# Gathering neighbour rows in a four-layer graph network: from bursts of tiles to pairs of transfers

## What is computed

```python
h = jnp.maximum(_layernorm(x, axis=-1), 0.0)   # before each layer
x = x + _L0_gnn_ref(h, adj, L0_gnn_kernel)     # normalised adjacency @ h @ W, relu
x = x + _L1_gnn_ref(h, adj, L1_gnn_W, L1_gnn_b)  # three propagations, then a linear layer
x = x + _L2_gnn_ref(h, adj, nodemask, ...)     # quantiles over the neighbours, then an MLP
x = x + _L3_gnn_ref(h, adj, L3_gnn_weight, L3_gnn_bias)  # adj @ (h @ W) + bias
```

```python
sv = jnp.sort(jnp.where(valid[..., None], x[:, None, :, :], big), axis=2)
for tau, wt in zip([0.25, 0.5, 0.75], [0.25, 0.5, 0.25]):
    pos = jnp.clip(tau * (mf - 1.0), 0.0)          # mf: number of neighbours
    agg += wt * (gather(floor(pos)) * (1 - frac) + gather(ceil(pos)) * frac)
```

## Time and profile before

| what | value |
|---|---|
| time, median of 3 runs | 2798.1 us (2797.18 to 2803.76) |
| the profiled execution | 2827.46 us, its span 2825.7 us |
| mean granted TensorE clock in it | 0.701 of full speed |
| busy: DVE, PE, Pool, PEld, ACT | 1625.1, 1535.0, 1299.3, 858.3, 462.6 us |
| Pool's gathers, L403 | 1152, 1287.4 us busy, 1118 ns mean |
| queue of the gathers (software) | 36864 packets, 37.82 MB |
| the chain of work that ended last | DVE 40%, PE 24%, "issue" 18%, unknown queue 15% |

### The profile page before, as it was taken

The page is one execution under the profiler, slowest core; times in us unless marked ns, Lnnn a source line. Parts: engine busy times, 40 slices in busy tenths (PEclk is TensorE's granted clock), DMA queues, the critical chain, the costliest instruction groups (busy, mean ns, idle before and its releaser), DMA issues.

```text
span 2825.7 us, 24253 instructions
## 1 busy us (share of the span) xinstructions
PE 1535.0 (54%) x8885; PEld 858.3 (30%) x8997; DVE 1625.1 (58%) x2443; ACT 462.6 (16%) x756; POOL 1299.3 (46%) x1196
## 2 busy tenths in 40 slices
PE   3735637556374655638366464836636375565232
PEld 2412414323142332314233241423314243233111
DVE  2511827649285574928467383755828376494926
ACT  3101212102021120202112020210302121020000
POOL 1072370735527173552717447172643707265550
PEclk9766658667586766759577676866768586777555
DMA  3122130313213131321313123131322313112120
GB/s 99 54 25 53 46 55 21 75 11 86 19 40 62 24 75 12 83 22 34 67 20 77 15 53 54 29 69 8 88 18 50 55 22 75 10 23 20 23 24 4
DMA packets 106610, 120.13 MB, mean 43 GB/s; under 512 B 71486, under 2 KB 71614, under 8 KB 106430
## 3 DMA queue, kind: packets, MB, share of 16 engines
q0 software_dynamic: 36864, 37.82, 14.2%
q1 hardware_dynamic: 69566, 79.98, 9.2%
HBM read 109.27 MB, written 8.45 MB: 42 GB/s over the span
## 4 chain that ended last, share of the span: by engine, by line
DVE 40%; PE 24%; issue 18%; another core or an unknown queue 15%; ACT 2%; DVEq 1%; POOL 0%; DMA 0%; POOLq 0%; ACTq 0%; SPq 0%
PE ps_tr L596 7%; DVE lists L1181 4%; DVE slots L1001 4%; PE ps_tr L604 4%; DVE slots L1000 3%; PE ps_prod L615 3%; PE ps_tr L585 2%; PE ps_misc L775 2%; DVE slots L1008 2%; DVE slots L1009 2%; DVE xc L977 1%; DVE stat L979 1%; DVE stat L976 1%; PE ps_misc L704 1%
## 5 line engine op out<-in xcount | busy, mean ns | idle before, releaser
L403 POOL DMA_INDIRECT slots<-h_rows,row_no x1152 | 1287.4, 1118 | 1433.2 <-DVEq L1187 1087.0
L596 PE MATMUL ps_tr<-adj_t,y_mid 128*128 128x512 bf16 x960 | 301.7, 459 | 223.7 <-issue 121.3
L1223 DVE TENSOR_TENSOR y_mid<-ps_prod,scales 128x512 f32<-128x512 f32 x48 | 33.2, 692 | 554.2 <-remote 407.5
L448 ACT ACTIVATE columns_t<-ps_tr 128x512 f32<-128x512 f32 (+1 forms) x192 | 113.0, 595 | 1409.2 <-PE ps_tr L604 888.7
L596 PEld LDWEIGHTS ps_tr<-adj_t,y_mid 128*128 128x128 bf16 x1024 | 105.6, 112 | 471.1 <-issue 416.0
L1181 DVE MAX8 lists<-ps_key 128x8 f16<-128x1024 f32 x128 | 157.8, 1233 | 112.8 <-PE ps_key L685 69.4
L585 PE MATMUL ps_tr<-h_t,w_l_sb 65*128 65x512 f32 x192 | 151.3, 896 | 107.6 <-issue 76.1
L695 PE MATMUL ps_misc<-parts_w,select_t 128*128 128x64 bf16 x384 | 36.7, 220 | 268.1 <-issue 229.3
L472 ACT ACTIVATE adj_n<-adj_f 128x1024 f16<-128x1024 f32 x128 | 134.3, 1050 | 229.1 <-remote 80.7
L604 PE MATMUL ps_tr<-adj_t,low 128*64 128x512 bf16 x1024 | 157.9, 419 | 16.9 <-issue 16.6
L615 PE MATMUL ps_prod<-both_ident,columns_t 128*128 128x64 f32 x768 | 107.9, 297 | 101.6 <-issue 91.6
(11 more groups left out here) (210 smaller groups left out, 2539.2 us busy)
## 6 DMA issues: line engine op xcount, KB each, us to landing
adj_f<-in_adj SPq DMA_DIRECT2D x128, 512.0 KB
slots<-h_rows,row_no POOLq DMA_INDIRECT x1152
x<-in_x SPq DMA_DIRECT2D x16, 256.0 KB
h_rows<-h SPq DMA_DIRECT2D x16, 256.0 KB, 2.9
out<-x SPq DMA_DIRECT2D x16, 256.0 KB
xc<-in_L_gnn_W SPq DMA_DIRECT2D x1, 64.0 KB
w_sb<-in_L_gnn_W SPq DMA_DIRECT2D x2, 32.0 KB
h_rows<-zeros SPq DMA_DIRECT2D x2, 32.0 KB, 1.5
```

What stands on the lines that cost most here:

```text
L403: pool.indirect_dma_start(out=slots[:, slot_of(par, s), t * C:(t + 1) * C], out_offset=None, in_=table[par][:, :], in_offset=bass.Indirect ...
L448: act.activation(dst, view, ACT.Copy, scale=scale).then_inc(tr_free, 1)
L596: nc.tensor.matmul(dst[:, :], top_halves(pair_of)[:, j, :], adj_t[g % 3][:, columns[j]], start=(j == 0 and not begun), stop=False)
```

## The change

Pool's transfers go to the two semaphores in pairs instead of in bursts of 14: two to the first, two to the second, and so on, through all 72 transfers of a graph, the wide ones too. Ahead of each pair Pool waits until the earlier pairs on the same semaphore have landed, that is, up to the last but one pair. So at most four transfers can be under way, where before it was up to 28. Each semaphore now counts 36 transfers a graph, and DVE's wait ahead of `sort_1` uses these numbers.

```diff
-    BURST_TILES = 2
-    GATHERS_OF = [(SLOTS - 1) * T // 2 + LIST, (SLOTS - 1) * T // 2]
+    PAIR = 2
+    GATHERS_OF = [((SLOTS - 1) * T + LIST) // 2] * 2
...
-                def row(column, s, t, k):
+                def landed(k):
+                    at_least(pool, gathered[par][k], issued[k] * 16)
+
+                def row(column, s, t):
+                    k = sum(issued) // PAIR % 2
+                    if sum(issued) % PAIR == 0:
+                        landed(k)
                     issued[k] += 1
...
                 for t in range(T):
-                    k = t // BURST_TILES % 2
-                    if t % BURST_TILES == 0:
-                        landed(k)
                     for s in range(1, SLOTS):
-                        row(t * SLOTS + s - 1, s, t, k)
-                landed(0)
-                row(COLS * SLOTS, 0, WIDE_A, 0)
+                        row(t * SLOTS + s - 1, s, t)
+                row(COLS * SLOTS, 0, WIDE_A)
                 for s in range(1, SLOTS):
-                    row(WIDE_A * SLOTS + s - 1, s, WIDE_A, 0)
+                    row(WIDE_A * SLOTS + s - 1, s, WIDE_A)
                 for s in range(SLOTS):
-                    row(WIDE_B * SLOTS + s - 1, s, WIDE_B, 0)
+                    row(WIDE_B * SLOTS + s - 1, s, WIDE_B)
```

More of the change, by code:

```diff
@@ L406, in row @@
                         .then_inc(gathered[par][k], 16)
-                def landed(k):
-                    at_least(pool, gathered[par][k], issued[k] * 16)
                 pool.wait_ge(rows_listed, g + 1)
```

## The result

The kernel after takes 2671.05 us in the median of 4 runs (2650.92 to 2697.45), the kernel before beside it 2800.93 us (2797.18 to 2816.76). The ratio is 0.9502, with a 95% interval from 0.9431 to 0.9573: faster by 5%. The forecast was 2817 us, slower by 19 us, in a range from 2750 to 2875 us. The case that came true is the rival "PE gets air", which I had given 0.20, and it was worth three times the tenth that I had priced.

A forecast was written before the change was run, and what follows sets the result against it. PE was taken to be held until Pool's gather ends, which bounds the turn. Late pairs at 1.1 us plus single late landings at 0.1 us, times 16 graphs, add 19 us to 2798: 2817 us, range 2750 to 2875.

The forecast's parts named there:

- PE gets air: Rival: gaps of Pool's waits or fewer queued transfers let PE through; 2757 us, at the far end 2391; chance 0.20.
- the tenth: A tenth of DVE's 407.5 us of waits for PE at the propagation's head gone: 41 us, giving 2757 us.
- A met wait costs nothing: On Pool, a wait inside a transfer whose condition has long been met adds 0 us to the usual 0.30 us.
- slower by much: Rival: each waiting pair on Pool loses 0.58 us of preparation, met or not; 316 us in all, 3114 us; chance 0.06.
- The allowance and its price: A pair's wait on Pool is free if the landing comes within 1.90 us; later landings cost 0.1 to 2.1 us.
- The sum: Pool's waits at late landings lengthen each gather by 1.2 us, over 16 graphs 19 us slower.
- The first graph: Sign: its gather on Pool ends 1 to 2 us later relative to its start than before (90.1 us).
- Whatever the gather gets longer while PE is held, the turn gets longer: The end of Pool's gather sets PE's release, 5 to 7 us behind it, so added gather time lengthens the turn.
- The last sign in the prediction: If the gather is longer but turns are not, the failing step is that the gather's end sets the release.
- Eight products of that size take 0.34 us: PE's products in the first turn, without a gather beside it, set against held ones of one per 2.80 us.
- The pace changes by 1 to 2%, and the gaps are short: Argument that Pool's waits slow its stream too little to let PE through.
- The far end: All of DVE's 407.5 us of waits for PE at the propagation's head gone: 2391 us.

The follow-up runs named there:

- e3_before: The kernel before, unchanged, traced on an occasion without the hold: 2097.65 us.
- e1_single: The kernel after, with one transfer in place of a pair, so at most two under way: 2386.33 us, ratio 0.8512 against before.
- e1_pace: The kernel before, with an unread memset on Pool ahead of every fourth transfer throughout the gather: 2385.49 us, ratio 0.853 by the medians.
- e6_early: The kernel before, with seven memset pauses of Pool among the first 28 transfers of each graph, none behind: 2737.13 us, ratio 0.9646.
- e1_spread: The kernel after, with empty list entries pointing at 128 different zero rows in place of one: 2725.75 us, ratio 0.9736 against before.

## Why the prediction was wrong, point by point

- **A met wait costs nothing: right.** Gaps of 0.30 us stand before all but some 50 of the 572 waiting transfers. The rival "slower by much" is out.
- **The allowance and its price: right in kind, too small.** The sum had 1.2 us a graph. The waits cost 1.8 us a graph beyond the usual 0.30 us gaps, and without the hold the gather grows by the same 1.8 us (105.5 to 107.3 us). I had set the late landings at the gather's end only. The rows have them also in the middle, at 834.43 for example. Just ahead of it (824 to 834 us) the DMA engines are 0.73 busy with 222 GB/s, and nearly all of it is SP's queue with the next adjacency tiles (queue: packets, MB, share of 16 engines, in that stretch):

```profile
q1 hardware_dynamic: 551, 2.02, 61.7%
q0 software_dynamic: 181, 0.18, 11.2%
```

  I had looked for a backlog of the gather and not for company.
- **The first graph: right.** Its gather takes 91.1 us (140.51 to 231.60) against 90.1 us, and it stays held.
- **"Whatever the gather gets longer while PE is held, the turn gets longer": this step failed.** Its first half, that the gather's end sets the release, held: the release still comes 3.0 to 4.6 us behind the end in 13 of 16 gathers. But a turn is the gather and what is left to do behind it, and the sum had only the first term, +1.2 us. The second it put at nothing, as if PE were always equally far when it is released. Measured, the gather grew by 3.8 us (103.0 to 106.8) and the rest shrank by 15.6 us (61.8 to 46.2), because the hold sets in later. The last sign in the prediction, that a longer gather with shorter turns would speak against the release, named the wrong half. The earlier trace rows pointed to the onset (4 transfers in ten us, PE free; 9 transfers, PE held).
- **"Eight products of that size take 0.34 us": a wrong pair of rows.** The first row is of L658, with 2 columns, the held ones are of L695, with 64. The right row is that of e3_before, 24 products of L695 in 0.86 us. The reading that PE is held stands.
- **"The pace changes by 1 to 2%, and the gaps are short": the argument that kept "PE gets air" at 0.20.** The first half is true. What I missed is that there are two states, and that, as it seems, a pause has only to come ahead of the hold. With a tipping point, effects don't scale with causes, and pricing the case at "a tenth" was a guess with no row behind it. The far end, 2391 us, is where e1_single and e1_pace came to lie (2386 and 2385 us), but that is luck: without any hold before takes 2098 us, so it was not the far end.
- **The sum's sign holds where the hold is absent**, if anywhere: 1.0027 (0.9991 to 1.0063), where +19 us would be 1.009. That is no change; my reading is that 1.8 us more of gather are hidden in a turn of 119 us in which DVE, not Pool, has 55% of the chain.
- The range was too narrow for a kernel in which one unexplained stall holds 15% of the chain. An effect that I couldn't explain was treated as a constant.

## What to carry to other kernels

If the chain has long pieces of "issue" or of an unknown queue, their cause is the first thing to find, and a change that touches the suspect even slightly can move the time far beyond its own cost; give such cases a wide range on both sides. A back-to-back stream of indirect transfers on Pool should be tried with small pauses at the moments where another engine's work is due: seven memsets in the right place took 12% off, the same seven in another place 3.5%. And measure such a gain on more than one occasion: here the very same pair of kernels differs by 5% on one and by nothing on the other. No version that ran is known to be best on both: the pauses of e1_pace and the singles were not run without the hold, and early pauses cost 2% there. The seven pauses in the middle are the nearest to it: 12% off with the hold, and no clear cost without (1.0035, 0.9994 to 1.0075).

## What the runs showed of the hardware that I had not expected

- One kernel, unchanged, has two levels on different occasions: 2778 to 2841 us and 2079 to 2119 us, apart from three outliers (3068, 7257 and 2183 us), each level steady over all other runs of its occasion.
- In the held state PE starts one instruction in 1.40 us, weight loads and products alike, so that a product comes every 2.80 us, with nothing to wait for. Quarter-sized transfers don't change the period, and in the gather shown above neither do pauses of Pool once it has set in. The hold has a second form, in which PE stands in one piece (19.30 us in after, 34.52 us in e6_early).
- Transfers that read one and the same row of the table land slowly: in the earlier trace rows the last two drain for 4 us at 16 GB/s after the last issue. With 128 different zero rows the last one is through in the first 2 us, and the DMA engines are far less busy for it, 0.06 in place of 0.72. These are stretches of e1_spread around the end of the first gather:

```profile
228.00:233.00 5.00, 0.36 (x2) 0.21 (x2) 0.00 (x0) 0.00 (x0) 3.77 (x4) 0.50 0.09 26
233.00:235.00 2.00, 0.17 (x1) 0.10 (x1) 0.00 (x0) 0.00 (x0) 0.00 (x0) 0.50 0.06 16
235.00:237.00 2.00, 0.27 (x1) 0.00 (x0) 0.00 (x0) 0.00 (x0) 0.00 (x0) 0.50 0.00 0
```
